# Layer normalization taken in chunks through all its steps, in a six-layer float32 kernel on one Trainium2 core

## Reference

```python
x = x + 0.5 * moe(_layernorm(x))            # 64 experts of width 64, the 8 best of each token, and a shared one
x = x + head_attention(_layernorm(x))       # 16 heads of 8 features, softmax without a mask
x = x + 0.5 * moe(_layernorm(x))
x = x + 0.5 * recurrent(_layernorm(x))
x = x + decayed_attention(_layernorm(x))    # normalizes its input again (norm1), and once more before its MLP (norm2)
x = x + 0.5 * recurrent(_layernorm(x))

def _layernorm(x, axis=-1, eps=1e-05):
    m = jnp.mean(x, axis=axis, keepdims=True)
    v = jnp.var(x, axis=axis, keepdims=True)
    return (x - m) / jnp.sqrt(v + eps)
```

## Time and profile before

| | us |
|---|---|
| median of 3 runs (2938.41 to 2938.88) | 2938.75 |
| the profiled execution | 2941.29 |
| its span, first to last instruction | 2939.5 |
| TensorE busy in the span | 2611.5 (89%) |
| VectorE busy | 2318.1 (79%) |
| ScalarE busy | 1793.4 (61%) |
| GpSimd busy | 1266.6 (43%) |

### The profile page before, as it was taken

One profiled execution on the slowest core, in us unless ns is written; L12 is line 12 of the kernel. 1 busy time (PEld: TensorE's weight loads), 2 busy tenths in 40 slices (PEclk: granted clock), 3 DMA queues, 4 the chain that ended last, 5 costly groups with the idle time before them and its releaser, 6 DMA issues. The chain is left out here.

```text
span 2939.5 us, 36048 instructions
## 1 busy us (share of the span) xinstructions
PE 2611.5 (89%) x11635; PEld 1987.1 (68%) x11635; DVE 2318.1 (79%) x3342; ACT 1793.4 (61%) x2921; POOL 1266.6 (43%) x1271
## 2 busy tenths in 40 slices
PE   7899999978999999999999979999999883555688
PEld 5688888856666666666666658888888662343466
DVE  5787778758999999999999777787877547766555
ACT  3455555538888888888888635555555433344365
POOL 2466666653233323332332226666666303444300
PEclk8999999988999999999999989999999886777798
DMA  2565666633333333333333235666665000000000
GB/s 76 116 149 131 150 134 149 135 125 100 104 102 101 104 104 102 101 104 104 97 107 103 71 72 113 142 140 143 142 141 126 8 23 29 15 15 0 7 8 29
DMA packets 107564, 273.55 MB, mean 93 GB/s; under 512 B 30576, under 2 KB 35312, under 8 KB 107248
## 3 DMA queue, kind: packets, MB, share of 16 engines
q1 hardware_dynamic: 82576, 237.56, 32.3%
q0 software_dynamic: 24576, 33.62, 4.1%
q10 hardware_dynamic: 224, 0.07, 0.0%
HBM read 256.20 MB, written 10.75 MB: 91 GB/s over the span
## 5 line engine op out<-in xcount | busy, mean ns | idle before, releaser
L612 POOL TENSOR_TENSOR moe_experts_lo<-moe_experts_hidden,moe_experts_hi 128x512 fp32r<-128x512 f32 x512 | 662.0, 1293 | 341.0 <-ACT moe_experts_hi L550 340.8
L893 DVE TENSOR_TENSOR heads_e_lo<-heads_e,heads_e_hi 128x1024 fp32r<-128x1024 f32 x512 | 616.0, 1224 | 25.7
L727 POOL DMA_DIRECT2D heads_left<-heads_parts x512 | 306.8, 614 | 677.5 <-PE psum L781 612.0
L557 ACT ACTIVATE psum<-psum 128x512 f32<-128x512 f32 x512 | 298.0, 582 | 480.2 <-PE psum L90 480.2
L833 ACT ACTIVATE heads_e<-psum 128x1024 f32<-128x1024 f32 x512 | 520.0, 1023 | 107.0 <-PE psum L781 107.0
L584 DVE TENSOR_TENSOR moe_experts_weighted<-moe_spread,psum 128x512 f32<-128x512 f32 x512 | 351.2, 686 | 190.7 <-PE psum L90 186.4
L88 PE MATMUL psum<-heads_e_hi,heads_v_lo 128*128 128x512 f32 x1024 | 430.0, 420 | 18.1 <-DVE heads_u L859 18.1
L88 PE MATMUL psum<-moe_n_hi,moe_w_lo 128*128 128x512 f32 x1024 | 401.3, 392 | 4.4 <-PEq L54 4.3
L89 PE MATMUL psum<-heads_e_lo,heads_v_hi 128*128 128x512 f32 x1024 | 404.4, 395 | 0.0
L90 PE MATMUL psum<-heads_e_hi,heads_v_hi 128*128 128x512 f32 x1024 | 401.6, 392 | 0.0
L89 PE MATMUL psum<-moe_n_lo,moe_w_hi 128*128 128x512 f32 x1024 | 400.9, 392 | 0.0
(11 more groups left out here) (425 smaller groups left out, 4300.7 us busy)
## 6 DMA issues: line engine op xcount, KB each, us to landing
moe_spread<-moe_mask SPq DMA_DIRECT2D x128, 1024.0 KB, 9.9
heads_right<-heads_parts SPq DMA_DIRECT2D x512, 64.0 KB
heads_left<-heads_parts POOLq DMA_DIRECT2D x512, 64.0 KB, 2.5
heads_scale<-heads_inverse_copy SPq DMA_DIRECT2D x64, 512.0 KB, 3.6
moe_experts_raw<-in_gate SPq DMA_DIRECT2D x16, 256.0 KB, 11.5
moe_experts_raw<-in_up SPq DMA_DIRECT2D x16, 256.0 KB, 11.7
moe_experts_raw<-in_down SPq DMA_DIRECT2D x16, 256.0 KB, 11.6
heads_parts<-heads_e_hi SPq DMA_DIRECT2D x16, 256.0 KB, 3.0
```

The costliest lines, as they stand in the source:

```text
L557: act.activation(psum[:, GATE + p % 2, :], psum[:, GATE + p % 2, :], ACT.Silu).then_inc(silu_ready, 1)
L612: pool.tensor_tensor(lo[:, p, :], hidden[:, p % 2, :], f(hi[:, p, :]), ALU.subtract).then_inc(low_ready, 1)
L727: eng.dma_start(f(tile[row:row + 2 * HEAD, h % 2, :]), parts_dram[dims, order:order + 2, at]).then_inc(loaded[h % 2], 16)
L893: dve.tensor_tensor(e_lo[:, s, :], e[:, s % 4, :], f(e_hi[:, s, :]), ALU.subtract).then_inc(low, 1)
```

## The change

`layernorm` is written anew as one pass. For each chunk: PE multiplies by a new constant `center` (identity minus 1/128), so x minus its mean comes straight out of the matmul (bank `CENTERED`, 3 banks); ACT squares it from PSUM and copies it to a ring `centered` of 4 chunks; PE reduces the squares to 4 columns of variance (2 banks in turn); ACT takes the root of these 4 columns; DVE takes their reciprocal and multiplies it with the identity into a [128, 4 x 128] `diagonal`; PE multiplies `ones` by that, which spreads the scale over all partitions (bank `SCALE`, 3 banks); DVE multiplies. The transposition and the split rows go. Copies to DRAM, weight splits, low parts and their engines are as before. The constant `row_columns` goes and `center` comes.

```diff
+                def difference(c):
+                    if x_loaded:
+                        pe.wait_ge(x_loaded[c], 16)
+                    after(pe, centered_ready, c - BANKS + 1)
+                    pe.matmul(psum[:, CENTERED + c % BANKS, :], center, x[:, chunk(c)], start=True,
+                              stop=True).then_inc(difference_ready, 1)
...
+                def spread(c):
+                    pe.wait_ge(diagonal_ready, c + 1)
+                    after(pe, scaled_ready, c - BANKS + 1)
+                    pe.matmul(psum[:, SCALE + c % BANKS, :], f(ones), diagonal[:, c % 2, :, :].rearrange("p a b -> p (a b)"),
+                              start=True, stop=True).then_inc(scale_ready, 1)
+
+                for c in range(CHUNKS + 3):
+                    if c < CHUNKS:
+                        difference(c)
+                    if 1 <= c <= CHUNKS:
+                        variance(c - 1)
+                    if c >= 3:
+                        spread(c - 3)
...
+                def square(c):
+                    act.wait_ge(difference_ready, c + 1)
+                    after(act, variance_ready, c - 2)
+                    act.activation(squares[:, c % 3, :], psum[:, CENTERED + c % BANKS, :], ACT.Square).then_inc(squares_ready, 1)
+                    after(act, scaled_ready, c - RING + 1)
+                    act.copy(centered[:, c % RING, :], psum[:, CENTERED + c % BANKS, :]).then_inc(centered_ready, 1)
...
+                for c in range(CHUNKS + 4):
+                    if c < CHUNKS:
+                        square(c)
+                    if 1 <= c <= CHUNKS:
+                        root(c - 1)
+                    if keep is None and c >= 4:
+                        high(c - 4)
...
+                def diagonals(c):
+                    dve.wait_ge(deviation_ready, c + 1)
+                    dve.reciprocal(inverse[:, columns(c)], deviation[:, columns(c)]).then_inc(inverse_ready, 1)
+                    dve.wait_ge(inverse_ready, c + 1)
+                    after(dve, scale_ready, c - 1)
+                    dve.tensor_tensor(diagonal[:, c % 2, :, :], identity.unsqueeze(1).to_broadcast([P, PARTS_OF_CHUNK, P]),
+                                      inverse[:, columns(c)].unsqueeze(2).to_broadcast([P, PARTS_OF_CHUNK, P]),
+                                      ALU.mult).then_inc(diagonal_ready, 1)
...
+                for c in range(CHUNKS + 2):
+                    if c < CHUNKS:
+                        diagonals(c)
+                    if 1 <= c <= CHUNKS:
+                        scaled(c - 1)
+                    if keep is None and c >= 2 and c - 2 in VECTOR_LOWS:
+                        take_low(dve, "vector", c - 2)
```

More of the change, by code:

```diff
@@ L201, in variance @@
                     for q in range(PARTS_OF_CHUNK):
[L202 to L205, removed]
+                        last = pe.matmul(psum[:, VARIANCE + c % 2, q:q + 1], squares[:, c % 3, q * P:(q + 1) * P],
+                                         inv[:, 0:1], start=q == 0, stop=q == PARTS_OF_CHUNK - 1, skip_group_check=True)
@@ L206, in variance @@
                     last.then_inc(variance_ready, 1)
[L208 to L216, removed]
@@ L229, in _ @@
+                for c in range(CHUNKS + 3):
[5 more added lines that the diff above has]
+                        spread(c - 3)
             @block.scalar
             def _(act):
-                for c in range(CHUNKS):
-                    act.wait_ge(centered_ready, c + 1)
-                    after(act, variance_ready, c - RING + 1)
-                    act.activation(squares[:, c % RING, :], centered[:, c, :], ACT.Square).then_inc(squares_ready, 1)
@@ new lines, in root, with high @@
+                def root(c):
+                    act.wait_ge(variance_ready, c + 1)
+                    act.activation(deviation[:, columns(c)], psum[:, VARIANCE + c % 2, 0:PARTS_OF_CHUNK], ACT.Sqrt,
+                                   bias=eps).then_inc(deviation_ready, 1)
+                def high(c):
+                    act.wait_ge(normal_ready, c + 1)
+                    act.copy(n_hi[:, chunk(c)], normal[:, c % RING, :]).then_inc(high_ready, 1)
+                for c in range(CHUNKS + 4):
[5 more added lines that the diff above has]
+                        high(c - 4)
@@ L242, in _ @@
             @block.vector
             def _(dve):
-                for c in range(CHUNKS):
-                    dve.wait_ge(mean_ready, c + 1)
-                    dve.tensor_tensor(centered[:, c, :], x[:, chunk(c)], psum[:, MEAN + c % 2, :],
-                                      ALU.subtract).then_inc(centered_ready, 1)
-                dve.wait_ge(deviation_ready, 1)
-                dve.reciprocal(inverse[:, :, :],
-                               deviation[:, :].unsqueeze(1).to_broadcast([P, 2, COLUMNS])).then_inc(inverse_ready, 1)
@@ L257, in _, with scaled @@
+                def scaled(c):
                     if keep is None:
```

67 lines of the change are left out of this document (24 added, 43 removed).

## The result

The changed kernel takes 2917.49 us (median of 5 runs, 2912.0 to 2923.2) against 2938.88 us (median of 5): ratio 0.992, 95% interval 0.9908 to 0.9931. That is 21.4 us less, where 18.9 were forecast.

A forecast was written before the change was run, and what follows sets the result against it. Eight unoverlapped normalizations cost their full length, pass 1 bound by PE, norm1's pass 2 by VectorE. Gains 4.5 + 0.9 + 3.4 + 4.5 + 4.4 + 0 + 1.2 = 18.9 us gave 2919.9 us, range 2902 to 2936.

The forecast's parts named there:

- PE's turn: Each chunk in the new normalization: difference 0.85, variance 0.90 and spread 0.85 on PE, 2.60 us.
- 24.9 undisturbed: A normalization without waits for POOL: 20.8 + 1.7 + 2.4 = 24.9 us, against 27.2 before.
- Meetings with POOL, 1.0 us a normalization: Diagonals on VectorE wait for POOL's instructions; the stage grows by 1.0 us, leaving moe1, cell0, cell1 1.5 each.
- 2.3 without waits: Upper bound of the gain in each of moe1, cell0 and cell1, if no diagonal waits for POOL.
- VectorE has 2.5 and waits for POOL 0.8: 3.2, now the bound over PE: In norm1 and norm2, per chunk: 31.5 us against 36.0, gains of 4.5 and 4.4.
- heads: One diagonal waits for POOL's 4.53 us subtraction, delaying SP's copies: end at 32.4 against 35.8, gain 3.4.
- The row of 1.65 us: In norm1, gain and bias took 1.65 us beside POOL's 1.26 us subtraction; said to agree with the lock.
- POOL is the bound: In moe0, weight splits and five low parts on POOL end near where they did; gain 0.4, counted as 0.
- The clock from decay to norm1: decay now ends with 512-column matmuls, so norm1 no longer begins at half speed; gain 1.2 us.
- decay: Normalization without low parts or POOL: 24.3 us before, 23.4 after, gain 0.9.
- that rival: The mixed stream is granted 1.2 GHz, 21 us more a normalization at full length; chance 0.08, shared with an unseen stall.
- the rival with little waiting: Most waits on POOL fall into PE's slack in all stages; 31 us gained, 2908; chance 0.22 for 2900 to 2912.

The follow-up runs named there:

- the run with pieces: Experiment 5: changed kernel with every weight split on POOL in pieces of at most 512 columns; 2914.11 us, ratio 0.9915.
- experiment 2: Changed kernel with the spread's matmul issued twice with the same operands; 2958.5 us, ratio 1.006.
- experiments 2 and 3: 2: changed kernel with the spread's matmul issued twice, 2958.5 us; 3: changed kernel with squares rounded and summed by one-pass matmuls, 2898.4 us.
- Experiments 6 and 8: 6: changed kernel, all low parts on VectorE (2923.59 us) or POOL (2925.01 us); 8: kernel before, new normalization in norm1 and norm2 alone (2931.88 us).
- experiment 4: Changed kernel with a root of a constant ahead of the first square, so the root's table loads first; 2910.49 us, ratio 0.9892.
- rounded squares: Changed kernel with squares in the one-pass matmul format, 2898.4 us; with the root's table first as well, 2891.04 us, or 2892.22 us with POOL's splits in pieces.
- experiment 7: Kernel before with the new normalization in decay alone; 2939.54 us, ratio 1.0002.

## Why the prediction was right, and where not

The total was right, and the mechanism for five of the eight stages; the forecast for norm1, norm2 and moe0 named a bound that isn't there.

**PE's turn** is 2.61 us (forecast 2.60), the first spread comes 6.2 us after the start in moe1 of the run with pieces (about 6), and that normalization, with no low clock, lasted 24.8 us to its last low part (24.9 undisturbed). A second L216 adds 0.86 us to a turn (experiment 2), and L202 takes 0.85. The core of the sum stands, by experiments 2 and 3 also.

**Meetings with POOL, 1.0 us a normalization**, was the term mis-sized in moe1, cell0 and cell1: with 24.8 us nothing is left of it. The gain there is 2.3 to 2.4 each by cell1's and moe1's profiles and not 1.5; 2.3 without waits was the upper bound in the forecast. The waits are there (the diagonal's median is 0.86 to 0.94 us in these stages, for 0.69 alone), and PE's slack takes them whole.

**norm1 and norm2** failed at the step "VectorE has 2.5 and waits for POOL 0.8: 3.2, now the bound over PE". Two things were wrong. Its work was summed from durations of 0.69 us that follow one another after 0.60, so that a turn without a low part lasts 2.2; and waits were added to the mean of a turn though they hit single turns, which PE, itself at 2.61, outlasts. Experiments 6 and 8 show it: 6.1 to 6.4 us are gained in each, not 4.5 and 4.4. The error would have been avoided by asking of each wait how far ahead of its consumer the waiting engine is.

**heads** came out by its steps: one wait of over 4 us (4.78), the first low part late, first copy 15.5 us after the start, last 32.5 (forecast 32.4), -3.3 us. In "SBUF — State Buffer", section "Who interferes with whom", the Trainium skill states that wait as a lock for a whole instruction; the trace agrees, with 4.78 us beside 4.83, 1.61 when POOL's pieces were 1.26 us, and 0.69 for the instruction with one input in PSUM. The row of 1.65 us that the forecast took as a sign of it is another case, a `tensor_scalar` with one tensor input. The copies took 17.0 us from first to last (forecast 16.4), but not at their own pace, as the forecast had it: the chunks came no faster. What the forecast didn't see is that 1.2 us decide how many diagonals get past first (experiment 4), which made the stage 4 us shorter; with rounded squares the same edit gave 2.2 (32.69 to 30.48).

**moe0** failed at "POOL is the bound". The earlier trace rows show the end of its splits at 23.85, but not that it then idled 7.50 us, waiting for the second pass. Where an engine has the last instruction and a gap ahead of it, it isn't the bound. 2.6 us against 0.

**The clock from decay to norm1**: 1.2 forecast, 1.6 measured (experiment 7). **decay**: 0.9 and 0.9. The clock in the mixed stream is 1.00 from 4 to 24 us after the start, so that rival fell; but in a form that the text hadn't, stretches of 13.7 us behind a start, it is real.

**The total** was near in part by luck. The terms were 10 us too small (18.9 against 29.3 in the stages), and what made up for it was in no term: 1.0 given back in the layers between, and 6.9 by where the two profiled runs lie in their kernels' scatter. Part by part the rival with little waiting was nearer (31 us). Of the 6.9, 4.5 are the changed kernel's, whose median run is longer than its profiled one. Long stretches at the low clock are the largest difference between like stages that traces show. Neither profile of the changed kernel has one, five of its eight variants' profiles do; each costs 5 us more than a short one, and the ten runs of the changed kernel lie at 2911.5 to 2913.9 (five), 2917.0 to 2918.0 (four) and 2923.2, steps of about that size. For it: the run of 2923.2 had the lowest mean clock, 0.949. Against it: the runs near 2917.5 have no lower mean clock (0.952 to 0.953) than those near 2912 (0.951 to 0.954), where a long stretch in place of a short one would make 0.002 less. So this stays open.

## What to carry to other kernels

When a barrier-like turnaround is broken up into a pipeline, find the bound by each engine's work in a steady turn, and charge a wait on another engine only as far as it exceeds the lead over its consumer. Then look at the filling on its own: a table load, or a long instruction that another engine has to wait for, is free where the bound engine has work, and costs microseconds where the first few steps must get past it. And compare stage lengths only between stages that were granted the same clock.

## What the runs showed of the hardware

- After a pause of PE of 2.2 to 2.7 us ahead of a normalization the granted clock was full, or at 1.2 GHz for 3.4 us, or for 13.7 us, with the same work on PE (moe1: 25.63, 27.20 and 32.18 us). The cost is about half of the stretch, as PE is the bound. The long one came at 10 of 40 starts of new normalizations in heads, moe1 and the cells, and at none of 16 old ones; PE was busy during all of it.
- With full-precision squares the moment of the fall parts the two: in the ten long ones the clock fell 0.65 to 1.35 us after PE's first difference, in the thirteen short ones between 0.47 before it and 0.15 after. The moment alone doesn't decide it: three starts with rounded squares fell at 0.53 to 1.29 and five old ones at 0.61 to 0.78, and all had 3.4 us. Why, no run tells.
- The attention behind norm1, the same code in every kernel, took 318.0 to 321.3 us. With the new norm1 seven of eleven profiles stand at 321.0 to 321.3, with the old the three stand at 318.0, 318.6 and 319.8.
- Four sums over 128 columns, one-pass with two columns each, cost 0.45 us a turn, full-precision with one column each 0.90.
